# Half-batch 3: y scaled on ScalarE, gamma and residual on GpSimd, and new instruction orders

## The reference

```python
x = x + attn(layernorm(x))      # attn ends in: y = h + out ; (y - mu)/sqrt(var + 1e-6) * gamma + beta
x = x + ffn(layernorm(x))

# attn: q, k = elu(.) + 1, 16 heads of 8; k divided by its norm per head; (q k^T) v; @ Wo + bo
# ffn:  scores = layernorm(x) @ w_router ; the 768 best of the 1024 rows of a batch get
#       gelu(row @ w_block), the others stay as they are
```

## Time and profile before

| | us |
|---|---|
| median of 3 runs | 91.2 (91.19 to 91.83) |
| the profiled execution, its own time | 91.51 |
| its span, first to last instruction | 89.8 |
| busy: PE / DVE / ACT / POOL | 79.9 / 80.9 / 66.9 / 52.8 |
| last VectorE instruction ends | 86.8 |

### The profile page before, as it was taken

The page is one execution under the profiler, slowest core; times in us unless marked ns, Lnnn a source line. Parts: engine busy times, 40 slices in busy tenths (PEclk is TensorE's granted clock), DMA queues, the critical chain, the costliest instruction groups (busy, mean ns, idle before and its releaser), DMA issues.

```text
span 89.8 us, 2397 instructions
## 1 busy us (share of the span) xinstructions
PE 79.9 (89%) x816; PEld 68.4 (76%) x816; DVE 80.9 (90%) x258; ACT 66.9 (75%) x186; POOL 52.8 (59%) x79
## 2 busy tenths in 40 slices
PE   4998689999999999999999599999999797999700
PEld 1335656976797997999999599999998797779600
DVE  4368999999797897999999999999999999999960
ACT  5003599998999996753539799999799696998700
POOL 5265885989992997659770979769838400000000
PEclk9999999999999999999999999999999999999996
DMA  0899969970999999900000000000000000348456
GB/s 24 233 256 319 280 168 319 290 189 7 143 127 140 139 143 136 112 10 0 0 0 0 0 7 0 0 4 7 0 4 0 0 7 10 107 121 236 138 149 180
DMA packets 18113, 8.99 MB, mean 100 GB/s; under 512 B 819, under 2 KB 18102, under 8 KB 18102
## 3 DMA queue, kind: packets, MB, share of 16 engines
q1 hardware_dynamic: 13232, 6.49, 26.7%
q0 software_dynamic: 4160, 2.10, 21.5%
q10 hardware_dynamic: 710, 0.26, 1.1%
HBM read 4.66 MB, written 2.10 MB: 75 GB/s over the span
## 4 chain that ended last, share of the span: by engine, by line
PE 46%; DVE 41%; issue 4%; ACT 3%; DVEq 1%; POOL 1%; ACTq 0%
DVE beats L918 11%; PE bank L1219 7%; PE bank L1211 7%; PE bank L1152 6%; DVE xb_sb L886 5%; DVE x_sb L941 5%; DVE bn L893 4%; PE bank L1252 4%; PE bank L1228 4%; PE bank L1253 4%; PE bank L1188 3%; PE bank L1271 3%; DVE beats L927 2%; DVE bn L818 2%; DVE x_sb L853 2%
## 5 line engine op out<-in xcount | busy, mean ns | idle before, releaser
L918 DVE TENSOR_SCALAR beats<-s_row,s_col 128x1024 bf16<-128x1024 f32 (+7 forms) x32 | 15.5, 541 | 0.0
L595 ACT ACTIVATE norm_sb<-xb_sb,shift,gain 128x128 f32<-128x128 f32 x32 | 13.2, 507 | 2.7 <-DVE shift L847 2.7
L1252 PE MATMUL bank<-M_sb,qT 128*128 128x128 f32 x64 | 12.5, 277 | 0.0
L1253 PE MATMUL bank<-back,hT 128*128 128x128 f32 x64 | 12.4, 275 | 0.0
L413 POOL TENSOR_TENSOR r<-var,minus_half 128x4 f32<-128x4 f32 x8 | 8.1, 1025 | 5.8 <-DVE var L833 5.5
L400 POOL TENSOR_TENSOR k_sb<-k_sb,k_rnorm 128x512 f32<-128x512 f32 x8 | 9.3, 1252 | 2.7 <-DVE k_rnorm L801 2.7
L426 POOL TENSOR_TENSOR r<-var,minus_half 128x4 f32<-128x4 f32 x8 | 9.1, 1194 | 2.9 <-DVE var L839 2.9
L1252 PEld LDWEIGHTS bank<-M_sb,qT 128*128 128x128 f32 x64 | 9.7, 192 | 0.2 <-ACT M_sb L558 0.2
L1253 PEld LDWEIGHTS bank<-back,hT 128*128 128x128 f32 x64 | 9.7, 192 | 0.0
L588 ACT ACTIVATE x_sb<-bank,r 128x128 f32<-128x128 f32 x32 | 9.2, 383 | 0.2 <-DVE s_col L901 0.2
L1219 PEld LDWEIGHTS bank<-w_c,hT 128*128 128x128 f32 x56 | 6.9, 192 | 2.1 <-ACT hT L513 1.1
(11 more groups left out here) (132 smaller groups left out, 216.7 us busy)
## 6 DMA issues: line engine op xcount, KB each, us to landing
xb_sb<-in_L_attn_x_dram SPq DMA_DIRECT2D x4, 512.0 KB, 6.8
xb_sb<-beta_sb POOLq DMA_DIRECT2D x4, 512.0 KB, 8.4
x_sb<-in_L_attn_x_dram SPq DMA_DIRECT2D x7, 256.0 KB, 5.2
out_dram<-x_sb SPq DMA_DIRECT2D x7, 256.0 KB, 2.3
x_sb<-in_L_attn_x_dram SPq DMA_DIRECT2D x2, 128.0 KB, 2.7
out_dram<-x_sb SPq DMA_DIRECT2D x1, 128.0 KB, 2.4
out_dram<-x_sb ACTq DMA_DIRECT2D x1, 128.0 KB, 2.5
w_sb<-in_L_attn_Wq_dram ACTq DMA_DIRECT2D x1, 64.0 KB, 2.5
```

The lines of the kernel that those rows point to most:

```text
L595: last = nc.scalar.activation(norm_sb[:, t], xb_sb[:, t], ACT.Identity, bias=shift3[:, t:t + 1], scale=gain3[:, t:t + 1])
L918: nc.vector.tensor_scalar(beats[:, b % 2, J, P * J:T * P], s_row[:, b, P * J:T * P], s_J, None, ALU.is_le).then_inc(beats_done, 1)
L1252: nc.tensor.matmul(o, qT[:, u, t * P:(t + 1) * P], M_sb[:, b], start=True, stop=False)
L1253: last = nc.tensor.matmul(o, hT[:, u, t * P:(t + 1) * P], back[:], start=False, stop=True)
```

## The change

Group 3 gets a third way to x1, "U": ScalarE scales y by its root out of PSUM into norm_sb (scale_y, the four activations that stood unused in the kernel), GpSimd multiplies norm_sb by gamma (the new y_gamma) and adds x + beta (residual, as for group 0). VectorE has nothing of it. The bank of y(3) is free once ScalarE is through. All four lists are in a new order, and BANK_USES with them.

```diff
-    X1_BY = 'SGGGGGGG'
+    X1_BY = 'SGGUGGGG'
...
-                return (yr_done, x1_by_pool.index(n) + 1) if n in x1_by_pool else x1_set(n)
+                return yr_set(n) if n in x1_by_pool else x1_set(n)
...
+        x1_by_pool = [u for u in range(U) if X1_BY[u] in "STU"]
+        scaled_by_act = [u for u in range(U) if X1_BY[u] in "TU"]
+        gamma_by_dve = [u for u in range(U) if X1_BY[u] in "ST"]
+        gamma_by_pool = [u for u in range(U) if X1_BY[u] == "U"]
...
+            def y_gamma(u):
+                if u == gamma_by_pool[0]:
+                    pool.wait_ge(gamma_in, 16)
+                a = TH * u
+                pool.wait_ge(y_scaled, scaled_by_act.index(u) + 1)
+                nc.gpsimd.tensor_tensor(norm_sb[:, a:a + TH], norm_sb[:, a:a + TH],
+                                        gamma_sb[:].unsqueeze(1).to_broadcast([P, TH, D]), ALU.mult).then_inc(yr_pool, 1)
+
             def residual(u):
                 a = TH * u
-                pool.wait_ge(yr_done, x1_by_pool.index(u) + 1)
+                pool.wait_ge(*yr_set(u))
```

More of the change, by code:

```diff
@@ L459, in _ @@
             roots2(3)
-            roots3(0)
+            roots2(4)
             roots3(1)
-            roots2(4)
+            y_gamma(3)
+            residual(3)
             roots2(5)
+            roots3(2)
             gelu_sum(0)
+            roots2(6)
             gelu_sum(1)
-            roots3(2)
             roots3(3)
             roots3(4)
-            roots2(6)
+            gelu_sum(2)
             roots2(7)
-            gelu_sum(2)
             gelu_sum(3)
@@ L664, in _ @@
             seed_norms(3)
-            copy_hk(2)
             square_seed(3)
+            copy_wz()
+            copy_M(2)
             y_stats(2)
-            copy_M(2)
+            exp_q_half(7)
+            norm_sum(0)
+            copy_hk(3)
+            scale_y(3)
             copy_xT(0)
             copy_xT(1)
-            copy_wz()
-            norm_sum(0)
+            copy_xT(2)
+            copy_M(3)
+            norm_sum(1)
             gelu(0, 0)
@@ L1009, in _ @@
+            mask_vk(2)
+            y_gamma(1)
             variances2(1)
-            y_gamma(1)
-            key_sums(7)
+            x1_stats(0)
+            variances3(0)
+            key_norms(3)
+            residual(1)
+            y_gamma(2)
+            variances2(2)
+            y_stats(3)
+            affine3(0)
+            variances2(3)
             q_half(7)
-            residual(1)
-            key_norms(3)
-            x1_stats(0)
             x1_stats(1)
-            mask_vk(2)
@@ L1018, in _ @@
[L1018 to L1021, removed]
+            y_stats(4)
+            variances2(4)
             variances3(1)
-            variances2(3)
-            y_gamma(3)
             residual(2)
-            residual(3)
-            affine3(0)
+            y_gamma(4)
+            x1_stats(2)
+            y_stats(5)
+            mask_vk(3)
+            affine3(1)
+            residual(4)
+            y_gamma(5)
+            variances3(2)
@@ L1028, in _ @@
+            variances2(5)
             score_cols(0, 0)
-            y_stats(4)
-            x1_stats(2)
+            score_cols(0, 1)
+            score_cols(1, 0)
             x1_stats(3)
[L1032 to L1036, removed]
-            score_cols(1, 1)
[L1038 to L1042, removed]
-            affine3(1)
@@ L1044, in _ @@
-            mask_vk(3)
-            x1_stats(4)
+            x1_stats(4)
+            residual(5)
+            score_cols(1, 1)
+            y_stats(6)
+            variances3(3)
+            variances2(6)
+            y_gamma(6)
             x1_stats(5)
-            variances3(3)
+            residual(6)
+            affine3(2)
+            score_cols(2, 0)
             variances3(4)
+            score_cols(2, 1)
+            variances3(5)
+            variances2(7)
             compare(0, 0, 1)
@@ L1051, in _ @@
             compare(0, 2, 1)
[L1052 removed]
             compare(0, 3, 1)
             compare(0, 4, 1)
[L1055 to L1061 removed]
+            mask_own(0, 0)
+            score_cols(3, 0)
+            score_cols(3, 1)
+            y_gamma(7)
+            x1_stats(6)
+            compare(0, 5, 1)
             compare(0, 6, 1)
             compare(0, 7, 1)
[L1064 to L1068 removed]
+            compare(1, 0, 1)
             mask_own(0, 1)
+            variances3(6)
+            residual(7)
+            drop_first(0)
             score_cols(4, 0)
[L1071 to L1075 removed]
             compare(1, 1, 1)
@@ L1096, in _ @@
             mask_own(1, 1)
+            merge(1)
+            score_cols(7, 0)
             compare(2, 1, 1)
+            score_cols(7, 1)
             compare(2, 2, 1)
@@ L1100, in _ @@
             compare(2, 4, 1)
+            drop_first(1)
+            mask_own(2, 0)
             compare(2, 5, 1)
+            affine3(7)
             compare(2, 6, 1)
             compare(2, 7, 1)
-            score_cols(6, 1)
-            drop_first(0)
-            score_cols(7, 0)
-            score_cols(7, 1)
-            merge(0)
-            mask_own(2, 0)
+            compare(3, 4, 1)
+            gelu_sum(5)
             mask_own(2, 1)
+            merge(2)
             drop_last(1)
-            gelu_sum(5)
-            drop_first(1)
-            compare(3, 4, 1)
             compare(3, 5, 1)
@@ L1371, in _ @@
             transpose_h(1)
+            q_proj(0)
             k_proj(1)
-            q_proj(0)
             transpose_h(2)
```

316 lines of the change are left out of this document (152 added, 164 removed), and 15 rows, old and new, of the table BANK_USES.

## The result

The changed kernel takes 94.2 us (median of 6 runs; 93.78 is the lowest) against 91.36 us for the kernel before (6 runs, 91.19 to 91.83). The ratio is 1.030, with a 95% interval of 1.026 to 1.034. Runs over 1.5% above the fastest of their kernel are left out of all ratios; here that is one of the six, of 105.7 us, with a TensorE clock of 0.757. The profiled execution took 93.78 us with a span of 92.0; that of before took 91.51 with a span of 89.8.

The account below looks back on a forecast made before the run. VectorE, never idle for a releaser from about 35 us to the last merge, was taken as the bound. Terms -1.63 + 0.3 + 0.3 - 0.6 + 1.0 + 1.15 + 1.25 = +1.77 us gave 93.0 us, range 90.0 to 94.6.

Parts of the forecast that it names:

- rival (1): The forecast itself, 93.0 us, with its own range of 92.1 to 94.4; chance 0.48.
- the late locks: Comparisons after about 57.5 us: GpSimd's gelu_sum(2) and gelu_sum(3) each stop VectorE, +1.15 and +1.25 us.
- Taken from VectorE: One 128x512 product and four residual pieces of half 3 leave VectorE: -1.63 us.
- Up to scale_y(0): Start to about 35 us: new waits, mainly 1.2 us at variances2(0), make scale_y(0) late by 0.3 us.
- Rival (3): The part before scale_y(0) loses nothing, y_full(0) before 32.0 us, locks as before: 89.6 us; chance 0.15.
- mask_vk(2): After scale_y(0): mask_vk(2) and y_gamma(2) wait for PE and the squares of half 2, +0.3 us.
- The chain of half 3: x1 of half 3 through ScalarE and GpSimd reaches x1_stats(3) with 0.9 us in hand: price zero.
- Rival (4): Half 3 is late by over its 0.9 us slack, so x1_stats(3) stands: 94.6 us; chance 0.15.
- The old variance: Variance of half 2 at 41.30 us, drawn out beside a key scaling before, becomes plain: -0.6 us.
- The middle locks: About 41 us to the first comparison: GpSimd may hold variances2(2), affine3(0) to (2), variances3(3); a third of 3.2, +1.0 us.
- Rival (2): The two late gelu sums find no comparison to hold: 90.6 us; chance 0.22.
- the signs named: Expected in the trace: three comparisons (or a mask) near 1.2 us, about 1 us wait at variances2(0), none at x1_stats(3).

Follow-up runs that it names:

- the last pair of runs: Changed kernel, y_half(0) before attention_matrix(1) on TensorE, y_stats(0) before exp_q(6) on ScalarE; the second also moved copy_hk(1) behind exp_q(6): 96.88 and 96.41 us.
- Root first: Changed kernel with roots2(7) moved in front of gelu_sum(2) on GpSimd: 92.85 us, ratio to before 1.013.
- additions on VectorE: Changed kernel with gelu_sum(2), (3) and (4) done by VectorE instead of GpSimd: 92.93 us.
- the second kernel with y_half(0) first: Changed kernel, y_half(0) before attention_matrix(1) on TensorE, y_stats(0) before exp_q(6) and copy_hk(1) behind exp_q(6) on ScalarE: 96.41 us.

## Why the prediction was right

The forecast was 93.0 us; 94.2 is within the range (90.0 to 94.6) and its own range (92.1 to 94.4), and rival (1), the forecast, is what happened. The mechanism that it rests on, the late locks, is what the runs showed; one term, that of the first stretch, came out right by luck. Step by step, on the profiled execution:

- **Taken from VectorE**, -1.63: the lines show one product and four pieces fewer, as said, with 0.6 and 0.9 us less of busy time. The starts give 0.61 + 1.03 = 1.64.
- **Up to scale_y(0)**, +0.3: it starts at 35.73 in place of 35.32, +0.4. The forecast waits were 0.8, 0.45 and 1.2; the trace has

```profile
22.83 1.28 DVE L812 TENSOR_REDUCE k_ssq<-k_sb 128x64 f32<-128x512 f32 x2 [0.70 <-ACT k_sb L554]
...
28.46 0.29 DVE L833 TENSOR_TENSOR vk_sb<-bank,head_mask 128x128 f32<-128x128 f32 x1 [0.73 <-PE bank L1252]
...
34.27 0.17 DVE L853 TENSOR_SCALAR var<-y_sq 128x4 f32<-128x4 f32 x1 [1.11 <-ACT norm_sb L584]
```

  and y_half(0) at 31.09 (forecast 31.0). The size was right and the reason mostly wrong: of the 1.8 us by which y_half(0) is later than in the earlier trace rows, the matrix in front of it accounts for 0.3, and the bank behind k_half(6) would have held it until 30.8 anyway, as the last pair of runs showed. That the term fits is luck. Rival (3) fell too: y(0) was full at 33.0, where it needed 32.0.
- **mask_vk(2)**, +0.3: a wait of 0.27.
- **The chain of half 3**, price zero: scaled at 46.87 (forecast 46.6), GpSimd from 47.18 to 49.80 (47.2 to 49.8), and x1_stats(3) at 50.43 without a wait. Rival (4) fell.

```profile
45.72 1.15 ACT L593 ACTIVATE norm_sb<-bank,r 128x128 f32<-128x128 f32 x4
...
47.18 1.28 POOL L430 TENSOR_TENSOR norm_sb<-norm_sb,gamma_sb 128x512 f32<-128x512 f32 x1
48.53 1.27 POOL L437 TENSOR_TENSOR xb_sb<-norm_sb,xb_sb 128x512 f32<-128x512 f32 x1
...
50.43 1.41 DVE L913 BATCH_NORM_STATS2 bn<-xb_sb 128x6 f32<-128x256 f32 x4
```

- **The old variance**, -0.6: it is gone, variances2(2) takes 0.16 us.
- **The middle locks**, +1.0: they came to 1.39, spread otherwise than weighed. affine3(0) took 0.30 of 1.2, affine3(1) at most 0.05, affine3(2) nothing, and variances3(3) 1.09, where I had bounded it at 0.6. That bound was the mis-sized term. It came from the clock of my hand schedule, in which the variance would start half way through the addition. A hold can last nearly the whole operation (1.09 of 1.27 here), so each of the four should have had 1.2 above, and a third of 4.8 would have been 1.6.
- **The late locks**, +1.15 and +1.25: the first comparison starts at 57.56 (forecast 57.5), gelu_sum(2) at 59.65 meets compare(0,4), gelu_sum(3) meets the first of group 1: +1.06 and +1.10. gelu_sum(4) holds one comparison as before, (1,5). Root first and additions on VectorE both gave 1.3 us back, so these holds are a cause and no mere coincidence. Rival (2) fell. Of the signs named, one is off: the held comparisons lasted 1.4 to 1.8 us, not near 1.2, since most of a comparison's own time comes on top.
- **The end** had its cover: no wait among the last merges.

The terms as measured (the first as forecast): -1.63 + 0.41 + 0.27 - 0.60 + 1.39 + 1.06 + 1.10 = +2.00, against +1.77. VectorE's last merge ends at 89.27 in place of 86.82, +2.45. Of the remaining 0.45, 0.07 is gelu_sum(4)'s hold (1.04 for 0.97) and 0.16 are sixteen comparisons of 256, 640, 768 and 896 columns that lasted about 10 ns longer each; 0.2 stays open. The medians lie 2.84 apart rather than 2.27, as the profiled execution of after was the quickest of its six and that of before stands 0.15 above its median.

My opening sentence, that each 0.1 us spared behind 35 us moves the end by 0.1 us unless a new wait appears, was too generous: in the old orders new waits do appear, for TensorE and for GpSimd's roots, and the saving is gone.

## What to carry to other kernels

Before moving work from VectorE to GpSimd, list which VectorE instructions will run beside every large GpSimd operation, for all those that the new order shifts and not only the moved ones: here a microsecond was lost or won per pair, more than an addition costs on VectorE itself. Taking two such pairs out of the kernel before, one by moving an addition to VectorE and one by shifting a single line, brought 0.85 us. An engine with no idle time can have a second one close behind it that no list of waits shows; look at that one's busy share in the stretch in question before you count the saving. And work that is taken off an engine may have been what it did while another engine made its next operand (here a root of 1 us): look for what can stand in its place.

## What the runs showed that I had not expected

- GpSimd can be the one held: an addition of 1.27 us took 2.25 when it started among comparisons back to back, and gelu_sum(4) took 1.79 at 69.50 in the kernel after, started during a merge. Its roots too run longer beside comparisons: two in 2.80 us, against 1.98 for two in the middle of the kernel. The roots, for their part, did not hold the comparisons beside them: in the kernel before, three comparisons from 54.50, beside three roots from 54.21, took their plain 1.87 us together.

```profile
64.94 2.80 POOL L443 TENSOR_TENSOR r<-var,minus_half 128x4 f32<-128x4 f32 x2
```

- A merge under a mask (COPY_PREDICATED, 0.72 us) is held as comparisons are: 1.78 us beside an addition from 72.86, in the second kernel with y_half(0) first.

```profile
72.94 1.78 DVE L961 COPY_PREDICATED x_sb<-dropped,norm_sb 128x512 f32<-128x512 int32 x1
```

- A bank of PSUM that a later stage shares with an earlier one worked like an entry in the engine's list, as far as the trace and BANK_USES show, and was not visible in any list of orders: TensorE stood 1.31 us for it, in both runs, once what had covered it was moved.
